# A graph attention layer with a routed feed-forward net: the parts of the picks summed in PSUM, and two node groups multiplied on GpSimd

## The reference, cut to what matters

```python
e = leaky_relu(a_src[src] + a_dst[dst], 0.2)
m = segment_max(e, dst)
e = exp(e - m[dst])
denom = segment_sum(e, dst)
alpha = e / denom[dst]
out = segment_sum(xh[src] * alpha[:, :, None], dst)      # then a norm over all nodes, and the residual
```

## Time and profile before

| | before |
|---|---|
| median of 3 runs | 1942.99 us |
| lowest and highest | 1940.53 and 1944.68 us |
| the profiled execution | 1942.65 us |
| its span | 1940.7 us |
| busy: PE, DVE, ACT, POOL | 87%, 73%, 58%, 63% of the span |
| edge stage, first gather to last sum | 92.95 to 1215.03 us of the span |

### The profile page before, as it was taken

The page is one execution under the profiler, slowest core; times in us unless marked ns, Lnnn a source line. Parts: engine busy times, 40 slices in busy tenths (PEclk is TensorE's granted clock), DMA queues, the critical chain, the costliest instruction groups (busy, mean ns, idle before and its releaser), DMA issues. The chain is left out here.

```text
span 1940.7 us, 37977 instructions
## 1 busy us (share of the span) xinstructions
PE 1692.2 (87%) x10851; PEld 1186.6 (61%) x10851; DVE 1420.1 (73%) x3880; ACT 1118.9 (58%) x2445; POOL 1214.0 (63%) x1150
## 2 busy tenths in 40 slices
PE   7769898898988988889898888636999999999997
PEld 5546554554544545445454444634898988989896
DVE  7787777877778777787777878896666666666664
ACT  5666666766667666676676764771434344443443
POOL 1277777777777777777777776101465656666653
PEclk9979899999999999999999999875999999999999
DMA  5554556455464554545555443587233333323322
GB/s 165 174 147 125 141 144 165 119 156 157 141 166 119 155 158 141 166 124 151 157 142 165 123 132 92 168 283 176 37 52 50 49 53 48 52 47 53 48 43 34
DMA packets 142689, 233.62 MB, mean 120 GB/s; under 512 B 31127, under 2 KB 107553, under 8 KB 141313
## 3 DMA queue, kind: packets, MB, share of 16 engines
q0 software_dynamic: 62800, 147.54, 32.1%
q1 hardware_dynamic: 69765, 81.13, 13.4%
q10 hardware_dynamic: 9932, 2.52, 0.8%
HBM read 188.81 MB, written 43.15 MB: 120 GB/s over the span
## 5 line engine op out<-in xcount | busy, mean ns | idle before, releaser
L1072 POOL DMA_INDIRECT gather_ring<-node_table,src_slot x879 | 838.5, 954 | 268.1 <-issue 252.8
L1159 PE MATMUL bank<-ones 128*128 128x512 bf16 x1759 | 553.4, 393 | 76.9 <-ACT gather_ring L1234 65.9
L1193 PE MATMUL bank<-gather_ring,onehot 128*128 128x264 f32 x1758 | 566.7, 405 | 51.0 <-DVE gather_ring L1118 50.6
L1193 PEld LDWEIGHTS bank<-gather_ring,onehot 128*128 128x128 f32 x1758 | 294.8, 195 | 261.4 <-DVE gather_ring L1118 219.3
L1090 DVE TENSOR_TENSOR acc<-acc,bank 128x264 f32 x879 | 367.9, 419 | 18.7 <-PE bank L1193 17.5
L1118 DVE TENSOR_TENSOR gather_ring<-gather_ring,bank 128x256 f32<-128x256 f32 x879 | 359.5, 409 | 0.3 <-ACT bank L1233 0.3
L2037 POOL DMA_INDIRECT out_rows<-y,token_idx x105 | 202.7, 1931 | 216.1 <-DMA out_rows<-y,token_idx 148.9
L1159 PEld LDWEIGHTS bank<-ones 128*128 128x128 bf16 x1759 | 168.6, 100 | 220.7 <-issue 102.6
L2005 ACT ACTIVATE hid<-bank,cols 128x256 f32<-128x256 f32 (+1 forms) x448 | 209.8, 550 | 141.8 <-PE bank L1951 138.9
L1951 PE MATMUL bank<-xe,w_hi 128*128 128x256 f16 (+1 forms) x1792 | 284.2, 267 | 0.6 <-ACT hid L2005 0.5
L1968 PE MATMUL bank<-w,hid_hi 128*128 x1680 | 278.3, 273 | 0.0
(11 more groups left out here) (287 smaller groups left out, 2056.0 us busy)
## 6 DMA issues: line engine op xcount, KB each, us to landing
w_stage<-in_L_ffn_W SPq DMA_DIRECT2D x16, 1024.0 KB, 7.2
dst_row<-dst_rows SPq DMA_DIRECT2D x110, 128.0 KB, 3.3
gather_ring<-node_table,src_slot POOLq DMA_INDIRECT x879
w_split<-w_out SPq DMA_DIRECT2D x32, 256.0 KB, 2.9
w<-w_split SPq DMA_DIRECT2D x8, 1024.0 KB, 13.8
node_table<-acc SPq DMA_DIRECT2D x24, 264.0 KB
xt<-in_x SPq DMA_DIRECT2D x24, 256.0 KB, 3.0
r_ring<-in_x SPq DMA_DIRECT2D x6, 896.0 KB, 10.6
```

The costliest lines, as they stand in the source:

```text
L1072: e.indirect_dma_start(out=gather_ring[:, b % GB, j, :], out_offset=None, in_=node_table, in_offset=bass.IndirectOffsetOnAxis(ap=src_slot[ ...
L1159: e.matmul(idle_bank[:, :].rearrange("p (k n) -> p k n", k=2), halves[:, 0:P], halves.rearrange("p (a n) -> p a n", a=1).broadcast_to([P, ...
L1193: e.matmul(bank[AGG[s % len(AGG)]][:, 0:ROW], onehot[:, b % OHB, j, :], gather_ring[:, b % GB, j, :], start=True, stop=True).then_inc(summ ...
```

## The change

TensorE makes the picks of a slot with three products of 16 columns that accumulate in PSUM, instead of one of 48 columns; the reduction on VectorE and its result `picked` go, and the score reads the bank itself. The wait for the picks and the bias sum (`vector_w1_bias`) move from `sum_picks` into `score`. The multiplication of the sixth and the seventh node group goes to GpSimd, behind its gathers and ahead of `pool_iotas`; a new semaphore `inverted` counts the reciprocals, which stay on VectorE.

```diff
-        picked = early.take("picked", [P, 2, EB, PICK])
...
-        normalised = sem("normalised")
+        inverted, normalised = sem("inverted"), sem("normalised")
+        POOL_DIVIDES = GROUPS - 2
...
-        W_AT = EB * 3 * PICK
+        W_AT = EB * PICK
...
         def pick_bank(b):
-            return bank[PICKS[b % 2]][:, 0:W_AT].rearrange("p (j i c) -> p j c i", i=3, c=PICK)
+            return bank[PICKS[b % 2]][:, 0:W_AT].rearrange("p (j c) -> p j c", c=PICK)
...
+        def multiply(e, g):
+            e.wait_ge(inverted, g + 1)
+            rows = acc[:, tiles(g), 0:D].rearrange("p n (h d) -> p n h d", d=DH)
+            e.tensor_tensor(rows, rows, acc[:, tiles(g), D:ROW].rearrange("p n (h a) -> p n h a", a=1)
+                            .broadcast_to([P, NG, HEADS, DH]), ALU.mult).then_inc(normalised, 1)
...
-            def sum_picks(b):
+            def score(b):
                 e.wait_ge(picks_done, b + 1)
-                vector_order.of(e.tensor_reduce(picked[:, b % 2, :, :], pick_bank(b), AX.X, ALU.add))
                 vector_w1_bias(e, b)
-
-            def score(b):
                 e.wait_ge(gathered[b % GB], 16 * (EB * (b // GB) + len(slots_in(b))))
-                e.wait_ge(vector_order.sem, vector_order.n)
...
                 vector_order.of(e.tensor_tensor(zbuf[:, 0, :, :], gather_ring[:, b % GB, :, D:ROW],
-                                                picked[:, b % 2, :, 0:HEADS], ALU.add))
+                                                pick_bank(b)[:, :, 0:HEADS], ALU.add))
...
-                vector_order.of(e.tensor_tensor(zbuf[:, 0, :, :], zbuf[:, 1, :, :], picked[:, b % 2, :, HEADS:PICK],
+                vector_order.of(e.tensor_tensor(zbuf[:, 0, :, :], zbuf[:, 1, :, :], pick_bank(b)[:, :, HEADS:PICK],
                                                 ALU.max))
...
             def divide(g):
                 e.wait_ge(added, final_at(g))
-                vector_order.of(e.reciprocal(acc[:, tiles(g), D:ROW], acc[:, tiles(g), D:ROW]))
-                e.wait_ge(vector_order.sem, vector_order.n)
-                rows = acc[:, tiles(g), 0:D].rearrange("p n (h d) -> p n h d", d=DH)
-                e.tensor_tensor(rows, rows, acc[:, tiles(g), D:ROW].rearrange("p n (h a) -> p n h a", a=1)
-                                .broadcast_to([P, NG, HEADS, DH]), ALU.mult).then_inc(normalised, 1)
+                e.reciprocal(acc[:, tiles(g), D:ROW], acc[:, tiles(g), D:ROW]).then_inc(inverted, 1)
+                if g < POOL_DIVIDES:
+                    multiply(e, g)
...
-            sum_picks(0)
...
-                if b + 1 < BATCHES:
-                    sum_picks(b + 1)
...
                 for j in range(EB):
-                    made = e.matmul(bank[PICKS[b % 2]][:, j * 3 * PICK:(j + 1) * 3 * PICK],
-                                    onehotT[:, b % 2, j * P:(j + 1) * P],
-                                    pick_parts[:, bass.ds(tile_regs[e.engine, b][j], 1), :, :]
-                                    .rearrange("p a i c -> p (a i c)"), start=True, stop=True)
+                    for i in range(3):
+                        made = e.matmul(bank[PICKS[b % 2]][:, j * PICK:(j + 1) * PICK], onehotT[:, b % 2, j * P:(j + 1) * P],
+                                        pick_parts[:, bass.ds(tile_regs[e.engine, b][j], 1), i, :]
+                                        .rearrange("p a c -> p (a c)"), start=(i == 0), stop=(i == 2))
                 made.then_inc(picks_done, 1)
...
             pool_edges(e, range(GB, BATCHES))
+            for g in range(POOL_DIVIDES, GROUPS):
+                multiply(e, g)
             pool_iotas(e)
```

## The result

| | before | after |
|---|---|---|
| median | 1943.84 us (4 runs) | 1990.71 us (4 runs) |
| lowest and highest | 1940.53 and 1945.75 us | 1987.14 and 1994.07 us |
| the profiled execution, its span | 1942.65, 1940.7 us | 1994.07, 1992.3 us |
| last sum ends, in the span | 1215.03 us | 1264.92 us |

The ratio is 1.0241, with an interval of 1.0227 to 1.0255. The forecast was 1939.7, in a range to 1944.0. Of the 51.6 us between the two spans, 49.9 are lost before the last sum; what follows it takes 727.4 us, against 725.7.

The account below looks back on a forecast made before the run. GpSimd's gather queue was taken to bound the edge stage, with VectorE mattering only near its end. Gains 2.0 + 0.7 + 0.6 = 3.3 us off 1942.65, plus 0.34 for the median, gave 1939.7; range 1936.5 to 1944.0.

Parts of the forecast that it names:

- What bounds the kernel now: Edge stage: GpSimd's gather queue bounds it at 10.08 us a batch; VectorE matters only in the last six batches and the end.
- The two multiplications: End of edge stage: sixth group's multiplication leaving VectorE gains 2.0 us, the seventh's nothing; GpSimd takes both at no cost.
- TensorE's picks become 24 products: Every batch: adds 0.9 to 2.1 us to TensorE's 7.29, staying under GpSimd's 10.08; no cost on the path.
- the late sums vanish in the 1.8 us: Clock rival, steady batches: sums delayed by the lower clock are covered by VectorE's 1.8 us wait for gathers.
- the clock falls more often: Rival, chance 0.2: thin picks lower TensorE's clock, delaying VectorE in batches 104 to 108; only 2.0 us gained, 1941.0.
- TensorE becomes the bound: Rival, chance 0.08: in every steady batch, picks not issued ahead push TensorE past 10.08 us; near 2005.
- p: Time per pick in the TensorE rival: 7.29 - 0.43 + 24 x p passes 10.08 at 0.134 us.
- the 0.43 us row: Profile row: weight loads of 8 picks took 0.43 us with TensorE behind; cited against TensorE becoming the bound.
- The reductions and batch 108: Late edge stage: dropping VectorE's reductions gains 0.7 us at stretched gathers; less TensorE idle time in batch 108 gains 0.6.
- The four stretched gathers: Batches 104 to 107: gathers lengthened by VectorE's multiplication, 5.33 us in all; expected near 4.6 after the change.
- What would show it wrong: Signs: idle time before gathers ending with TensorE's sums, transposes waiting for GpSimd, edge-stage granted clock well below before's.

Follow-up runs that it names:

- thin run: Kernel before with two more 16-column products ahead of each pick, each with its own register step, into an unread bank: 1996.65 us, ratio 1.0266.
- changed kernel with fixed rows: Changed kernel with the second and third part of every pick read from a fixed row, without a register: 1940.95 us, ratio 0.9987.
- fixed-row run: Kernel before with two more 16-column products ahead of each pick, the added ones reading a fixed row without a register step: 1945.54 us, ratio 0.9997.

## Why the prediction was wrong

**What bounds the kernel now** was read rightly, and so was the place where TensorE stood to it: 7.29 us a batch, cover to 10.08.

**The two multiplications** came as forecast: 2.0 us off VectorE (8.04 us from the last score to the end of the last sum, 8.2 said), GpSimd 3.21 us each (2.02 to 5.4 said, 3.7 taken), and by itself this half gained 2.3 us. By the Trainium skill, "GPSIMD Engine Reference", section 3.1, the estimate was 3.9; the trace has 3.21.

**The step that failed** is "TensorE's picks become 24 products": "Cost on the path: nothing; cover 0.7 to 1.9 us". Its price per pick was right: 0.06 to 0.13 us, measured 0.105; 8.2 to 9.4 us a batch, measured 9.48 on average at the upper clock, just over the top of it. What it left out is that half of the batches are not at the upper clock after such a stretch. The row for that was quoted, 3.71 us for nine wide products behind products of one column, and used in the rival on the clock; but there its cost in the steady batches was waved off with "the late sums vanish in the 1.8 us". That slack is VectorE's wait for gathers. The 1.7 us (3.79 - 2.10) fall on TensorE, whose cover was by then 0.5 to 0.7: 9.5 + 1.7 = 11.2 us, measured 11.06, and with half of the batches so, and eight of 13 to 15 us, the mean is 10.49 and passes 10.08. The two rivals, "the clock falls more often" (0.2) and "TensorE becomes the bound" (0.08, near 2005), were priced each as if the other did not happen. It was the second, set off by the first: p never reached 0.134 us (0.119 at most), the point from which it was said to decide. The argument against it, the 0.43 us row (TensorE is fast when it is behind), held for 8 picks and not for 24. In the thin run the first six of one set came 0.03 us apart and the other eighteen 0.125 (605.99 to 606.17, then to 608.42); that TensorE's queue works only so far ahead fits this, but was not tested by itself.

**The reductions and batch 108.** The gains of 0.7 and 0.6 can't be read in the changed kernel, where GpSimd has done its gathers 30 us before the end. In the changed kernel with fixed rows they could show, and its profile has neither. The four stretched gathers take 2.01, 2.04, 2.53 and 2.57 us, 5.3 us more in all than four of 0.95, the same as in the kernel before. Batch 108, from score to multiplication, and TensorE's first product in it:

```profile
1194.85 0.22 DVE L1105 TENSOR_TENSOR zbuf<-gather_ring,bank 128x64 f32<-128x64 f32 x1 [3.98 <-DMA gather_ring<-node_table,src_slot]
...
1203.62 2.03 DVE L1086 TENSOR_TENSOR acc<-acc 128x1792 f32<-128x1792 f32 x1
```

```profile
1196.43 0.58 PE L1156 MATMUL bank<-ones 128*128 128x512 bf16 x1 [4.45 <-ACT gather_ring L1231]
```

It takes 1203.62 - 1194.85 = 8.77 us, 1.0 longer than the 7.76 before: TensorE had been idle 4.45 us there, not 3.24, and the granted clock from 1190 to 1200 us is 0.76, not 0.83. (The set of picks ahead of it takes 1.1 us, hardly more than the 0.94 of the kernel before, so it can't take the forecast 1 to 2 us off the idle time.) That run's whole gain, 2.5 us (0.9987), is that of GpSimd's multiplications alone (2.3 us), within the intervals.

**What would show it wrong** was named rightly: a granted clock below before's in the edge stage (0.91 against 0.96), and more idle time before gathers that ends with TensorE's sums (49.4 us against 12.2).

## What to carry to other kernels

Cutting one product into several with the same columns in all costs TensorE little if their addresses are fixed (0.025 us each here, 0.105 with a register step for each); look in the profile for a register step per instruction before you take a short row for their price. On an engine with a clock that follows its work, ask of every thin stretch what the instructions behind it will cost at the lower level, and add that to the engine's own batch, not to the slack of another engine. Filler products (the wide ones that nobody reads) do more among thin instructions than behind them: there they hold the clock (0.96 for the edge stage in the place of 0.91) and hide the register steps (3.55 us a set in the place of 4.6).

## What the chip showed that was not expected

- 16-column products at a fixed address went by 0.025 us apart (24 in 0.61 us); with a register step for each, 0.105. The Trainium skill, "TensorE: Matmul & The Clock Gate", Part 1, has about 25 ns as the least from start to start of small products; the fixed-row run agrees.
- Leaving out four of nine wide products made those left slower: five took 2.18 us, where nine had taken 2.10 in every second batch, and the stage's clock went from 0.91 to 0.82.
- The lower clock came after half of the thin stretches, mostly after every second one: 52 of 104 in the changed kernel's profile, and 52 of 104 when it ran again.
- Two chips took 2202 and 2222 us for the kernel before. The products added to the picks cost 15 to 17% there, and 0 to 2.7% on the other chips. What holds the engines up there stays open.
